# The second attention product moved ahead of the convolution's matmuls in its slot

## What is computed

```
z   = _ln_c(x)                                   # normalised over channels
qkv = conv1d_same(group_norm(z), qkv_w, qkv_b)   # 16 taps, 256 -> 768 channels
w   = softmax(einsum('bct,bcs->bts', q * scale, k * scale))   # 4 heads of 64
h   = einsum('bts,bcs->bct', w, v)
x   = x + z + conv1d_same(h, proj_w, proj_b)     # 5 taps
t   = tokens(x);  n = _ln_t(t)
out = t + n + (table look-up on n, added to 32 of its columns)
```

## Time and profile before

| | us |
|---|---|
| median of 3 runs | 1107.07 (1104.65 to 1107.1) |
| profiled execution | 1104.99 |
| its span | 1103.2 |
| TensorE matmuls busy | 987.4 (90%) |
| VectorE busy | 716.3 (65%) |
| ScalarE busy | 650.2 (59%) |
| GpSimd busy | 233.4 (21%) |
| mean granted TensorE clock | 0.965 of full speed |

### The profile page before, as it was taken

One profiled execution on the slowest core, in us unless ns is written; L12 is line 12 of the kernel. 1 busy time (PEld: TensorE's weight loads), 2 busy tenths in 40 slices (PEclk: granted clock), 3 DMA queues, 4 the chain that ended last, 5 costly groups with the idle time before them and its releaser, 6 DMA issues.

```text
span 1103.2 us, 18112 instructions
## 1 busy us (share of the span) xinstructions
PE 987.4 (90%) x7250; PEld 684.0 (62%) x7250; DVE 716.3 (65%) x1222; ACT 650.2 (59%) x1049; POOL 233.4 (21%) x164
## 2 busy tenths in 40 slices
PE   2888649999999999999598999999999999988864
PEld 1555526667766776667366666766677668766654
DVE  5988557654775577668466555465536665777767
ACT  4673617664676477767565565465636575665532
POOL 2736122100330132124050000010001004313320
PEclk9998879999999999999799999999999999999987
DMA  7050033593459357737644284537445873453522
GB/s 272 13 180 1 1 125 65 99 212 68 91 111 247 51 118 168 165 67 146 171 77 86 47 185 106 87 63 182 93 67 110 201 167 73 97 124 59 115 58 77
DMA packets 284515, 122.59 MB, mean 111 GB/s; under 512 B 268304, under 2 KB 270736, under 8 KB 283536
## 3 DMA queue, kind: packets, MB, share of 16 engines
q1 hardware_dynamic: 284432, 121.44, 49.5%
HBM read 34.24 MB, written 15.87 MB: 45 GB/s over the span
## 4 chain that ended last, share of the span: by engine, by line
PE 59%; DVE 11%; ACT 8%; issue 7%; DMA 2%; POOL 1%; SPq 0%; ACTq 0%; POOLq 0%; DVEq 0%
PE cM L1049 15%; PE cQ L1049 14%; PE cP L1049 13%; PE psT L1118 4%; PE psV L1095 4%; PE psS L1118 4%; PE psV L1099 3%; ACT arena L909 2%; DVE smx L1495 2%; DVE W L1280 1%; DMA arena<-arena 1%; DVE arena L1472 1%; PE cM L990 1%; ACT arena L921 1%; PE cP L990 1%
## 5 line engine op out<-in xcount | busy, mean ns | idle before, releaser
L1049 PE MATMUL cP<-U,W 128*128 128x256 f16 (+1 forms) x1536 | 224.3, 303 | 13.8 <-DVE W L1280 12.5
L1049 PE MATMUL cM<-U,W 128*128 128x256 f16 (+1 forms) x1536 | 223.3, 301 | 11.4 <-DVE U L1309 7.4
L1049 PE MATMUL cQ<-U,W 128*128 128x256 f16 (+1 forms) x1536 | 225.6, 302 | 5.7 <-DVE W L1280 3.5
L1049 PEld LDWEIGHTS cP<-U,W 128*128 128x128 f16 x1536 | 150.7, 98 | 82.0 <-issue 11.6
L1049 PEld LDWEIGHTS cM<-U,W 128*128 128x128 f16 x1536 | 149.6, 98 | 81.1 <-issue 8.9
L1049 PEld LDWEIGHTS cQ<-U,W 128*128 128x128 f16 x1536 | 149.7, 98 | 74.2 <-issue 6.0
L1472 DVE SCALAR_TENSOR_TENSOR arena<-arena,smx 128x1024 f16<-128x1024 f32 x128 | 178.5, 1394 | 1.3 <-ACT arena L921 0.6
L902 ACT ACTIVATE smx<-smx,esc 128x1 f32<-128x1 f32 x128 | 37.5, 293 | 207.4 <-DVE smx L1495 207.0
L921 ACT ACTIVATE arena<-arena,smx 128x1024 f16<-128x1024 f32 x128 | 147.0, 1148 | 4.2
L1495 DVE TENSOR_REDUCE smx<-psS 128x1 f32<-128x1024 f32 x64 | 77.9, 1217 | 71.5 <-PE psS L1118 71.1
L1495 DVE TENSOR_REDUCE smx<-psT 128x1 f32<-128x1024 f32 x64 | 78.0, 1219 | 57.1 <-PE psT L1118 56.7
(11 more groups left out here) (212 smaller groups left out, 1202.1 us busy)
## 6 DMA issues: line engine op xcount, KB each, us to landing
staging<-w_qkv SPq DMA_DIRECT2D x20, 512.0 KB, 5.1
kept_u<-U SPq DMA_DIRECT2D x4, 2077.0 KB, 10.0
U<-kept_u SPq DMA_DIRECT2D x16, 519.2 KB, 4.4
arena<-x_tok SPq DMA_DIRECT2D x8, 512.0 KB, 6.4
arena<-arena SPq DMA_DIRECT2D x16, 256.0 KB, 3.8
W<-x_tok SPq DMA_DIRECT2D x4, 1024.0 KB, 6.1
out_tok<-W SPq DMA_DIRECT2D x3, 1024.0 KB, 4.3
kept_h<-arena SPq DMA_DIRECT2D x4, 514.0 KB, 4.2
```

What stands on the lines that cost most here:

```text
L1049: last = mm(out, W[:, j, wl, c, wat + tap, :], U[:, slot, ul, c, at:at + width], start=(c == 0 and tap == 0 and wl + ul == 0), stop=(c == ...
```

## The change

The call of `second_product` for the even slots 4 to 16 stands before the convolution (or the projection tiles) of its slot. In slots 4 to 14 that is right behind the scores; slot 16 has no scores, so there the product is the slot's first work. The waits inside the call move with it. The call for h = 7 stays.

```diff
                         last.then_inc(S["s_done"], 1)
+                    if attn and 4 <= i <= 16 and i % 2 == 0:
+                        second_product(k, i // 2 - 2)
                     if conv:
...
                             if kind == "tile":
                                 project(e, *tile)
-                    if attn and 4 <= i <= 16 and i % 2 == 0:
-                        second_product(k, i // 2 - 2)
                     if attn and not conv and i == 17:
```

## The result

The changed kernel is slower: median 1139.13 us of 4 runs (1134.98 to 1139.51) against 1106.84 us before, ratio 1.0288, 95% interval 1.026 to 1.0315. In a second comparison on another chip it took 1137.93 us against 1105.29, ratio 1.0297 (1.0282 to 1.0312). The profiled execution has a span of 1133.2 us, 30.0 more than before.

A forecast was written before the change was run, and what follows sets the result against it. TensorE, busy without a gap in middle steps, was taken as the bound, so waits add in full. 23.5 + 1.0 + 3.8 + 0 = 28.3 us gave 1133.3 from the profiled execution; forecast 1134 us, range 1126 to 1145.

The forecast's parts named there:

- what sets the end: End of heads_sum is set by a chain from scores 7 through the softmax work, 6.90 us, not by the product.
- terms 2 to 4: Slots 8, 12 and 16: products h = 2, 4, 6 stall TensorE for heads_sum by 1.41, 1.36 and 1.14 us.
- Term 5: The three stalls don't cover each other: 3.91 us a step, 23.5 us over n = 1, 2, 3, 5, 6, 7.
- Term 6: Odd products and h = 0 wait only for DMA transposes; slot 6 of n = 2 stalls 1.0 us, bounds 0 and 3.
- Term 7: Later convolution results delay half_y in slot 10: 0 in quiet steps, up to 1.5 us each in n = 2 to 4.
- Term 8: Step n = 4: group 0's copy 2.2 us late, slot 16's half_y adds 1.6; 3.8 us, bounds 1 and 7.
- Term 9: Last step: products wait 6 us for heads_sum, tiles come 3.3 us later, covered; 0 us, bounds −3 and +7.
- Signs: Trace: some 21 more psV waits for heads_sum, quiet steps 3.9 us longer, n = 4's 11.8 us maximum wait replaced.
- A: Later VectorE work comes due in loaded steps and partly the last step: 40 us, about 1142 to 1146; chance 0.13.
- B: Each TensorE pause drops the clock: 18 slow stretches of 1.5 us, 27 us more, 1161; chance 0.05.
- C: Not slower: psV free in time, heads_sum chain ending 1.41 us earlier, 5.5 us instead of 6.90; 1101 to 1105; chance 0.05.
- D: Stalls partly taken up by unseen slack, or fewer of the three slots late: 1118 to 1126; chance 0.07.

The follow-up runs named there:

- The run with early reading: Changed kernel with psV read out earlier: heads_out ahead of the exponential, heads_sum right behind the maximum; 1100.16 us against 1106.14 for the kernel before.
- the one with the first item ahead: Changed kernel with all seven products behind the convolution's first item (last step: first half tile) instead of ahead of it; 1112.84 us against 1106.14 for the kernel before.

## Why the prediction was right, and where not

- **Bound, chain and place (what sets the end; terms 2 to 4): right.** Predicted stalls 1.41, 1.36 and 1.14 us; the matmuls moved by 1.41, 1.36 and 1.15. Quiet steps got longer by 3.92 and 3.91 us against 3.91. The run with early reading shows the cause, the one with the first item ahead the size.
- **Term 5, sum over six steps: right.** 23.5 us predicted for n = 1, 2, 3, 5, 6, 7. Measured 3.67 + 3.73 + 3.92 + 3.91 + 4.30 for the five without n = 2, 19.5 in all where 19.6 was predicted. Only the quiet steps n = 5 and 6 show the term cleanly, and that the five meet the sum to 0.1 us is partly luck. The slot 16 waits of n = 3 and 7 are longer than the quiet step's 0.99 us (1.57 and 1.36), in slot 16 of n = 3 a wait of 0.51 us of the kernel before (L998, for a weight maximum) is gone, and n = 1 repeats to 1.4 us only (115.72 us in the second execution of the changed kernel).
- **Term 6, the transpose in n = 2: right, with a neighbour overlooked.** 0.84 us of idle time behind the DMA, 0.99 us for the step with odd products alone. n = 2 as a whole took 5.93 us, the terms had 4.9. The missing 1 us is in slot 8: 2.26 us of idle time where the quiet step has 1.25. I had counted this step as a quiet one.
- **Term 7, the cover for half_y: right in the quiet steps, wrong in n = 4,** as its bound allowed: "up to 1.5 us" was 1.04 for slot 10.
- **Term 8, step n = 4: mis-sized, 3.8 predicted, 5.67 measured, inside its bounds of 1 and 7.** The late copy of group 0 was near (2.2 against 2.5), though with the other six moved that part came to nothing more. The estimate for slot 16, 1.6 us "from the length of one product", was 4.4 with that product alone moved. It left out that the product's own pause stands ahead of half_y as well: half_y then has to wait for heads_sum, the product and 24 matmuls in a row, in part at the lower clock. And slot 12's stall, though taken up, cost 1.2 us by the clock.
- **Term 9, the last step: right.** Predicted 0; moved alone, 179.84 against 179.63 us. In the changed kernel the waits were 7.58, 4.08 and 4.48 us rather than 6 each, and the products behind them ran slow (1.86 us where 1.03 is usual, for the first), all without cost.
- **Sum.** 28.3 us against 30.0 between the profiled executions; n = 2 and n = 4 are short by 1.0 and 1.9, the last step gave 1.1 back. By the medians the change costs 32.3 us, 2.3 more than by the profiled executions. So the median of 1139.13 lies 5.1 us above the forecast 1134, inside the range; part of that distance is this unexplained 2.3 us, not a term.
- **Signs.** As foretold, 21 waits of psV for heads_sum are added to the 3 of before, and in n = 4 the wait of 11.84 us for the maximum is gone, with one of 11.88 us in front of a product in its place.
- **Rivals.** A came true in n = 4 alone. B did not for pauses up to 1.57 us: of the 17 waits for heads_sum between 0.99 and 1.57 us in the convolution steps none has a slow product or slow matmuls right behind it, in either profiled execution of the changed kernel. It did for one of 2.26 us, in one execution of two. C fell with the chain, still 6.89 us long. D fell in the quiet steps, which paid the stalls in full. The run with early reading adds that psV could be freed earlier, but by moving its reader, not the product.

## What to carry to other kernels

Before an operation is moved up in an in-order queue, list each semaphore that it waits for and write the time at which each is given beside the new place; here one subtraction per slot gave 3.91 us a step and 3.92 came out. If the consumer is to go earlier, move the release of its buffer first: with the reader of psV ahead of the long softmax work the same move cost nothing in quiet steps, and the reader's move alone was worth 0.9%. Where that gain comes from was only argued: a wait at the head of a loaded engine's queue seems to cost even where the engine waited for, here ScalarE, isn't the bound.

## What the runs showed of the hardware

A pause of TensorE of 0.99 to 1.57 us never slowed the matmuls right behind it (17 in each of two executions). Longer ones did or didn't, and their length alone does not sort them. Pauses of 2.26 to 2.28 us were followed by full speed in two places of the first execution of the changed kernel. The first of them, 2.26 us, was followed by the lower clock in the second execution, at a cost of 1.6 us, and one of 2.27 us in n = 4 with only h = 2, 4 and 6 moved also had a slow product behind it (1.87 us). In n = 4 of both executions of the changed kernel the product behind 3.23 us was slow and that behind 3.29 us was not. One of 3.27 us was followed by 12 matmuls in 1.54 us in the kernel before, and one of 3.25 us by 12 in 2.72 us with slot 12 alone moved. From the end of the VectorE instruction to the start of the waiting matmul it was 0.15 us in the quiet step too (674.93 + 0.68 = 675.61, start 675.76), and 0.14 to 0.16 us in all 24 waits for heads_sum in both executions of the changed kernel.
